# Another merged order of two halves of a six-layer decoder, with the instructions and their waits kept

## The reference

```python
x = _layernorm(x + _L0_attn_ref(x, ...))        # causal attention, one head of 256
x = _layernorm(x + _L0_xattn_ref(x, ctx, ctx, mask, ...))   # masked cross attention, a layernorm inside
x = _layernorm(x + _L0_ffn_ref(x, ...))         # three matmuls with weights of +1 and -1, 1024 hidden
x = _layernorm(x + _L1_attn_ref(x, ...))        # Performer: relu features, running sums, 16 heads
x = _layernorm(x + _L1_xattn_ref(x, ctx, ctx, ...))         # mLSTM with gates, 8 heads
x = _layernorm(x + _L1_ffn_ref(x, ...))         # quantized matmuls, a 3-tap convolution, silu, 1024 hidden
```

## Time and profile before

| what | value |
|---|---|
| median of 3 runs | 925.19 us |
| the runs | 925.56, 917.60, 925.19 us |
| span of the profiled execution | 919.4 us |
| one overlapped stretch | 204.6 us |
| PE, DVE, ACT, POOL busy | 85%, 62%, 40%, 16% of the span |

### The profile page before, as it was taken

How to read it: one execution, slowest core, us unless ns; L and a number is a source line. 1 busy time by engine, 2 the same in 40 slices (tenths; PEclk the granted TensorE clock), 3 DMA queues, 4 the chain that set the end, 5 groups by cost and what they waited for, 6 DMA issues and landing times.

```text
span 919.4 us, 14911 instructions
## 1 busy us (share of the span) xinstructions
PE 782.6 (85%) x5987; PEld 522.8 (57%) x6036; DVE 574.4 (62%) x1430; ACT 368.4 (40%) x654; POOL 147.3 (16%) x228
## 2 busy tenths in 40 slices
PE   8789977899999887899999887799999887859294
PEld 5554535666675544666665645666765654638142
DVE  1653733335875768645865778636865778666666
ACT  2563121125551165335641156235641265253052
POOL 4110010001222300001322200001412200024200
PEclk9998999999899999999999999999999999989596
DMA  9410000020010000020010000020010000000000
GB/s 360 155 46 1 0 21 4 2 70 24 1 46 1 1 24 2 2 91 24 1 47 1 1 24 2 2 68 1 2 47 1 1 1 2 1 24 2 0 0 24
DMA packets 13524, 25.87 MB, mean 28 GB/s; under 512 B 784, under 2 KB 7056, under 8 KB 13200
## 3 DMA queue, kind: packets, MB, share of 16 engines
q1 hardware_dynamic: 13456, 24.92, 7.8%
HBM read 22.82 MB, written 2.10 MB: 27 GB/s over the span
## 4 chain that ended last, share of the span: by engine, by line
PE 65%; DVE 20%; ACT 8%; issue 4%; another core or an unknown queue 2%; POOL 1%; DVEq 0%; ACTq 0%; POOLq 0%
PE bank L990 12%; PE bank L831 8%; PE bank L839 5%; PE bank L882 3%; PE bank L1000 3%; PE bank L1085 3%; PE bank L1293 3%; PE bank L978 3%; PE bank L862 2%; DVE work L1698 2%; PE bank L1033 2%; PE bank L1332 2%; PE bank L1067 1%; DVE work L1961 1%
## 5 line engine op out<-in xcount | busy, mean ns | idle before, releaser
L2287 POOL TENSOR_TENSOR rstd<-rstd,minus_half 128x2 f32<-128x2 f32 x56 | 44.3, 793 | 467.7 <-DVE rstd L1424 467.7
L990 PE MATMUL bank<-work,f0w 128*128 128x512 f16 x512 | 111.7, 379 | 0.0
L990 PEld LDWEIGHTS bank<-work,f0w 128*128 128x128 f16 x512 | 50.2, 98 | 59.6
L2115 ACT ACTIVATE work<-bank 128x512 f16<-128x512 f32 x64 | 37.9, 597 | 113.5 <-PE bank L990 93.9
L1617 DVE SCALAR_TENSOR_TENSOR work<-bank,work 128x512 f16<-128x512 f32 x64 | 42.9, 688 | 42.0 <-ACT work L2115 41.9
L1501 DVE TENSOR_REDUCE small<-bank 128x1 f32<-128x512 f32 (+3 forms) x32 | 18.6, 583 | 65.1 <-PE bank L863 51.1
L882 PE MATMUL bank<-work 128*128 128x256 f32 x208 | 49.8, 383 | 1.8 <-ACT work L2053 1.8
L817 PE MATMUL bank<-bar_upper,identb 128*128 128x512 bf16 x104 | 32.0, 424 | 19.9 <-DVE x L1433 8.4
L2153 ACT ACTIVATE work<-bank 128x512 f32<-128x512 f32 x32 | 18.9, 592 | 67.7 <-PE bank L1085 67.7
L1085 PE MATMUL bank<-work 64*128 64x128 f32 x512 | 38.1, 289 | 5.6 <-issue 4.0
L882 PEld LDWEIGHTS bank<-work 128*128 128x128 f32 x208 | 38.2, 190 | 7.7 <-ACT work L2053 2.3
(11 more groups left out here) (279 smaller groups left out, 1766.4 us busy)
## 6 DMA issues: line engine op xcount, KB each, us to landing
ctxT<-in_ctxT SPq DMA_DIRECT2D x8, 512.0 KB, 4.6
work<-in_mask SPq DMA_DIRECT2D x4, 1024.0 KB, 6.1
xT<-in_xT SPq DMA_DIRECT2D x4, 512.0 KB, 3.6
work<-in_w SPq DMA_DIRECT2D x1, 2048.0 KB, 18.7
ctx<-in_ctx SPq DMA_DIRECT2D x4, 512.0 KB, 3.9
perf_w<-in_perf_w SPq DMA_DIRECT2D x1, 1536.0 KB, 15.8
out<-y SPq DMA_DIRECT2D x3, 512.0 KB, 3.2
x<-in_x SPq DMA_DIRECT2D x2, 512.0 KB, 7.3
```

The costliest lines, as they stand in the source:

```text
L990: ins = nc.tensor.matmul(u.bank[:, :], f0w1[:, k, m * P:(m + 1) * P], h1[part][:, k, :], start=(k == 0 and part == 0), stop=(k == NF - 1 a ...
L2115: nc.scalar.activation(dst[0][:, m, :], u.bank[:, :], ACT.Relu).then_inc(high_made.sem, 1)
L2287: nc.gpsimd.tensor_tensor(s.rstd[:, two], s.rstd[:, two], minus_half[:, 0:2], ALU.pow).then_inc(s.rstd_made.sem, 1)
```

## The change

The three tables get other numbers, and with them an order of turns: in the changed kernel a number is the place of the step in a period of 189 turns, and both halves start at a multiple of the period. The list of steps, the instructions of a step, its waits, the sequences of PSUM banks, SP's queue and the number of ACT's table loads (16) are the same. Front 0 alone and back 3 alone stand in the same order as before on PE and DVE. Two lines of each table, and the rest of the diff:

```diff
-    ("mlstm.raw1", 296, None, 318, None),
+    ("mlstm.raw1", 32, None, 36, None),
-    ("quant.down1", 1324, 1376, None, None),
+    ("quant.down1", 125, 178, None, None),
...
-PERIOD, LATER = 3914, 160
+PERIOD = 189
...
 def front_starts(b):
-    return 60 + b * PERIOD
+    return b * PERIOD
...
 def back_starts(b):
-    return 60 + (b + 1) * PERIOD + LATER
+    return (b + 1) * PERIOD
```

More of the change, by code:

```diff
@@ L53 @@
[L53 to L76, removed]
@@ L88 @@
[L88 to L99, removed]
@@ L159 @@
[L159 to L164 removed]
+    ("self.q", 1, None, 1, None),
+    ("self.v", 2, None, 2, None),
+    ("self.score0", 3, 2, 3, None),
+    ("self.ck0", 4, None, 4, None),
+    ("self.score1", 5, 4, 5, None),
+    ("self.score2", 7, 5, 7, None),
+    ("self.ck1", 6, None, 6, None),
@@ new lines @@
+    ("cross.bar0", None, 22, None, None),
+    ("cross.bar1", None, 23, None, None),
+    ("cross.bar2", None, 24, None, None),
+    ("cross.bar3", None, 25, None, None),
+    ("self.norm1", None, 21, 20, None),
+    ("cross.xT0", 18, None, 19, None),
+    ("cross.xT1", 21, 27, None, None),
+    ("cross.q0", 20, None, 21, None),
+    ("cross.score0", 24, 29, 24, None),
+    ("self.rstd1", None, None, None, 5),
+    ("cross.score1", 25, 32, 25, None),
+    ("cross.q1", 23, None, 23, 6),
+    ("cross.score2", 26, 33, 29, None),
@@ new lines @@
+    ("cross.in_norm1", None, 50, None, None),
+    ("cross.product3", 34, 48, 38, None),
+    ("cross.add1", None, 55, None, None),
+    ("cross.rstd0", None, None, None, 8),
+    ("cross.stats1", None, 58, None, None),
+    ("cross.norm0", None, 51, 44, None),
+    ("cross.in_rstd1", None, None, None, 9),
+    ("sign.xT0", 43, 59, 45, None),
+    ("cross.norm1", None, 62, 50, None),
+    ("sign.early", 48, None, None, None),
+    ("sign.xT1", 49, 66, 51, None),
+    ("sign.a0", 51, 71, 52, None),
@@ new lines @@
+    ("perf.fq.0", 85, 122, 79, None),
+    ("perf.xT0", 77, None, 75, 22),
+    ("perf.q.1", 88, None, 83, None),
+    ("perf.fk.0", 92, 129, 84, None),
+    ("sign.rstd0", None, None, None, 19),
+    ("perf.k.1", 93, 130, None, None),
+    ("perf.v1", 82, 120, None, 23),
+    ("perf.ft.0", 94, 132, 87, None),
+    ("perf.state.0", 96, 136, None, None),
+    ("sign.rstd1", None, None, None, 20),
+    ("perf.score0.0", 99, 138, 93, None),
+    ("perf.score1.0", 101, 141, 94, None),
+    ("perf.before.0", 100, None, None, None),
@@ L165 @@
+    ("perf.spread.1", 126, 180, 121, None),
+    ("perf.out0", 129, 186, None, None),
+    ("perf.out1", 130, 187, None, None),
 ]
 BACK_TIMES = [
-    ("mlstm.xT0", -29, None, 115, -554),
-    ("first.rstd0", None, None, None, -554),
-    ("first.rstd1", None, None, None, -554),
-    ("first.stats0", None, -242, None, None),
-    ("first.norm0", None, -242, -174, None),
-    ("first.stats1", None, -242, None, None),
-    ("first.norm1", None, -242, 115, None),
-    ("mlstm.xT1", -29, 86, None, None),
```

456 lines of the change are left out of this document (226 added, 230 removed).

## The result

The changed kernel takes 896.5 us in the median of 4 runs (894.4 to 898.0), the kernel before 925.1 (917.6 to 925.6). The ratio is 0.9727, with a 95% interval from 0.9688 to 0.9766: faster. This ratio is estimated from all the runs and is not the quotient of the two medians, which is 0.969. The median of the kernel before moves from series to series: in three later ones of 13 to 25 runs it was 919.6 to 920.6, in a fourth of 7 runs 925.2. In the profiled executions 919.4 us became 893.8, that is -25.6. The working gave -16.2, the forecast was 909: the direction was right, the gain was larger, and 896.5 lies only 0.5 us inside the range.

A forecast was written before the change was run, and what follows sets the result against it. PE's work was taken as fixed, so reordering could only touch its 21.4 us of non-busy time a stretch, partly paced by DVE. Terms summed to -5.6 a stretch, -16.2 in all: 903.2 profiled, 909 median; range 896 to 928.

The forecast's parts named there:

- The 0.28 before `out0`: mLSTM heads: PE's old wait for eight DVE products, used to argue that the 0.97 wait is moved, not saved: 0.
- The row that the prediction took as support: Stretch at 187 us: 0.5 us more PE busy time, yet 204.66 against 204.61, so PE's time doesn't set the heads' end.
- The -1.76 and the +0.5: Sign layer: PE's waits for `sign.norm1` (0.87) and `round0` (0.89) go; `perf.qk.0` then waits some 0.5 for DVE's `xT1` copy.
- the +0.7 for a late `b7`: Sign layer: moved work delays DVE's `b7` by 0.7 us, and `sign.c0` needs it at its end.
- the -2.5: First Performer group: PE's waits of 0.67 (`fq.0`), 0.53 (`state.0`) and 1.32 (`score0.0`) go, saving 2.5 us a stretch.
- it does not last: First Performer group: `conv7`, ahead of `score3.0` on DVE, gives back 0.9, so inverse and spread come 1.6 early, not 2.5.
- 0.72, 0.62 and 1.40: Stretch end: PE's waits before `score3.1`, the spread and `perf.out0`, covered by the four down-projections; sum -2.74.
- DVE's pace: Performer: moving conv steps only changes which engine waits, so both groups give nothing; -9.9 us, 915; chance 0.17.
- Gain lost at the boundary: Stretch boundary: PE runs ahead, then waits in the next for `first`, mask load or head products; about 922; chance 0.15.
- Slower: Five places where a 1.5 us DVE conv step precedes a front step PE awaits; +4.2 a stretch, 938; chance 0.11.
- The case of 895 us: PE's listed waits, 10.0 us a stretch and 30 in all, go without new ones; 895; chance 0.03.
- Clock: PE's early arrival at `out0` lowers the clock through `sign.a`; 1.7 us a stretch lost, 914; chance 0.02.

The follow-up runs named there:

- end: Kernel before, with the new order only in the second group of Performer heads and the end of the stretch; 0.9882 of the kernel before.
- performer: Kernel before, with the new order only in the first group of Performer heads, on PE, DVE and ACT; 0.9868 of the kernel before.
- later: Changed kernel, first Performer group: hidden3, hidden4 (PE) and conv2 (DVE) behind fk.0, conv7 (DVE) behind score3.0; 0.9696 of the kernel before.
- the four parts: Four runs of the kernel before, each with the new order in one place: heads 1.0001, sign layer 0.9994, first Performer group 0.9868, second group and stretch end 0.9882.
- later2: `later` with hidden7 ahead of score3.0 on PE, conv7 and top4 behind the inverse on DVE, conv8 and top5 later still; 0.9853 of the kernel before.
- performer_pe: Kernel before, with the first Performer group in the new order on PE alone, DVE and ACT as before; 1.0005 of the kernel before.
- performer_rest: Kernel before, with the first Performer group in the new order on DVE and ACT, PE as before; 1.0011 of the kernel before.
- turn1: `performer_pe` with one more step moved: DVE's copy of turn1 ahead of its product of fq.0; 0.9999 of the kernel before.
- sign: Kernel before, with the new order only from the end of the mLSTM heads to the first Performer projection; 0.9994 of the kernel before.

## Why the prediction came out as it did

By its own steps, for one stretch, from the parts without dips:

| step | predicted | measured |
|---|---|---|
| up to the first mLSTM output | 0 | -0.5 |
| sign layer to first projection | -0.6 | -1.25 |
| Performer, first group | -1.6 | -3.2 |
| second group (`topT`) | -0.8 | -0.9, less 0.3 given back |
| end of the stretch | -2.6 | -4.05 |
| sum | -5.6 | -9.5 |

**Heads.** The mechanism was right: the wait of 0.97 moved (to 1.15 before `head6`). The balance was off by 0.5. The 0.28 before `out0` that the prediction built on was read in a stretch with a clock dip at the heads. Where `end`, which has the old order there, had no dip, the wait for DVE's product is six times as long:

```profile
467.24 1.94 PE L1293 MATMUL bank<-work 128*128 128x66 f32 x16 [1.69 <-DVE work L1781]
```

So DVE's chain does set the end of this part, and the new order shortened that chain by 0.5. The row that the prediction took as support is no support: the first stretch took 205.7 us from its true start at 186.37, and 75.9 up to `out0` against 74.8 in the second, with a dip of 7 us at the heads instead of 3. PE at half clock for long enough does move the end.

**Sign layer.** The -1.76 and the +0.5 are as predicted (0.56 before `qk.0`, no wait before L1315). The failed step is the +0.7 for a late `b7`: L1000 doesn't wait. DVE began `b7` 0.88 us after PE began `c0` (500.13 and 499.25), before it was 0.83 (509.25 and 508.42): 0.05 late and not 0.7.

**First group.** Up to `score0.0` the -2.5 is right. `performer` shows -1.98, though `hidden7` now lies in that part; it had taken 0.53 behind `score0.0` (547.52 to 548.05). Like for like that is -2.5. The failed step is "it does not last". PE does wait 0.90 for the product behind `conv7`, but 0.20 of it stood there before, so `conv7` costs 0.70, and it was booked alone. `conv7` had to stand somewhere: in the kernel before it stood between the same product and the inverse. Taking it from there shortened the wait before the spread by 0.59; the one before the fourth block of scores fell by 0.55 and one of 0.17 went, as DVE no longer ran late there. Together that is -0.61. From `score0.0` to the spread the prediction has +0.9; the runs have -1.2, or -0.7 without `hidden7`. This one term is the whole 1.6 between -1.6 and -3.2.

**End.** Mis-sized terms: 0.72, 0.62 and 1.40 went as predicted, plus 0.17 inside `down0`, plus 0.32 before the denominators (0.52 to 0.20, by the q steps), which the working left out, plus the overlap of 0.17 at each wait. The 0.1 given back on DVE isn't seen.

**From the sum to the time.** The range held by 0.5 us, and that is in part luck: the sum for a stretch was too small by two fifths. Of the 12.5 us between 909 and 896.5, 9.4 are in the profile (25.6 against 16.2). The other 3.1 come from the base: 925.2 lies 5.8 above the span that was profiled, the new median 2.7 above its own. A run takes only some 1.2 us more than its own span (895.0 and 893.8); the rest is that the profiled execution of the kernel before ran at a clock of 0.959 while its runs of 925 us in the later series ran at 0.954 to 0.956.

**The rivals.** DVE's pace: refuted for the changed kernel, true one step beyond it (`later`). Gain lost at the boundary: refuted by the four parts. Slower: only `conv7` bites, as counted; `later2` shows what such steps can cost. The case of 895 us fits the time but not its reason: PE is idle for 13.8 us a stretch still, and waits of 0.56, 0.90 and 1.15 are new. Clock: in the way that was described it is out, since PE's arrival at `out0` costs a wait of 0.22 only and the second stretch has a share of 1.00. But its sign, a share below 1.00 between `sign.a` and the end, did come in the third stretch, with PE busy all the time:

```profile
757.70:761.10 3.40, 3.40 (x50) 2.98 (x50) 2.85 (x9) 1.12 (x2) 0.00 (x0) 0.50 0.02 5
```

It cost 1.6 us there, near the 1.7 that the rival put on a stretch. The last section says in which kernels it came.

**What the prediction never asked.** It took each move on PE at the wait that it fills. `performer_pe` and `performer_rest` show that neither engine's part is worth anything much without the other. The step that makes the fillers free, `turn1` on DVE, isn't among its terms, though it is in the change.

## What to carry to other kernels

A filler is worth the idle time it covers plus the overlap that the wait had cost (here about 0.17 us), if its inputs are there; follow them to the engine that makes them, since in the trace one copy behind the wrong product took back the whole gain of PE's moves. When a step moves on an engine that is nearly full, book both ends: the wait that it makes where it comes to stand, and the one that it leaves where it stood. And look for a small gain in the lengths of parts in the trace, but don't claim it for the time until the runs show it: gains of 3 to 4 us by lengths (`sign`, `turn1`) could not be shown in medians, nor by sorting runs by their mean clock.
